# Rough attention scores as pairs of 64-row tiles, and the weighted sums copied out of PSUM by ScalarE

## The chip, the cores and the metric

One core of a Trainium2 chip runs one program. The metric is the device time of one execution in microseconds (us), median of the runs shown.

## The reference, cut to what matters

A 7x7 local-attention convolution is followed by full attention over 3136 tokens of 64 features for each of 4 images, and then by gates and a mixture of experts. The change lies in the attention:

```python
scores = a[:, :, None] + b[:, None, :] + einsum('bif,bjf->bij', x * wc, x)
attn_weight = softmax(scores, axis=2)
attn = einsum('bij,bjf->bif', attn_weight, x)
```

with x the layer-normed tokens (4, 3136, 64). The softmax needs a number near each query's largest score, so that the exponentials stay in range; any such number gives the same quotient.

## The kernel before

`attention` splits the tokens of every image b into 7 chunks of 448 queries (CH) and 25 tiles of 128 keys (NT, the last of 64). Two float16 parts, high and low, stand for a float32 number: `xs` has the high part of the keys in partitions 0 to 63 and the low part in 64 to 127, `vh` and `vl` the projected queries, doubled over both halves of the partitions.

A **step** is one chunk; 28 of them run over 4 images, and one more (`body(B, 0, ...)`) ends the last. Step i does two things at once on TensorE. It makes **rough scores** (L959) of its own queries, whose largest values DVE takes (L1257); they are needed for the next step only. And it **attends** for chunk i-1: exact scores (L970, two matmuls for each key tile), exponential on ScalarE (L1088), weighted sums (L986, float32, two 64-column tiles side by side).

A step has 13 slots of two key tiles (SL). TensorE's order in a slot s: at odd s the sums of two earlier slots, then rough score, two exact matmuls, rough, two exact, and in some slots a third rough score. Steps with 4 query tiles (q = 0, 2, 4, 6 of an image) have 28 rough scores, e = 0 to 27, three to a slot; steps with 3 (q = 1, 3, 5) have 21, two to a slot. They end in slot 9. In slot 10 the maxima are transposed (L1048), in slot 11 the next image's queries are projected (L942; ScalarE L1068 and DVE L1148 copy them out); both use banks of `ps_m`, the 3 banks of the rough scores. Rough score e waits until DVE has reduced e-3; e = 2 waits for L1148 of the step before.

All sums of a chunk gather in one PSUM bank, `ps_a`. The last sums of chunk i-2 are issued in slot 1 of step i. DVE copies the bank out between its reductions (`block_out`, L1239), and the first sums of chunk i-1, in slot 3, wait for that copy:

```python
for back in range(s - LAG - s % 2, s - LAG + 1):
    for a in range(len(tiles(back))):
        sums(m, i - 1, back, a)
...
elif s == 0:
    pe.wait_ge(sums_out, n)
```

SP then gathers the denominators from the copy and moves one half (`denominators`), DVE inverts (`invert`, L1243, L1245), and GpSimd multiplies (`finish`). `steps` runs steps 2 to 5 of an image in a hardware loop.

Of the kernel before, what the change touches and what calls it, by code (L numbers as in the profile page):

```python
# [20 lines left out]
PIX = H * W  # L21
# [623 lines left out]
def attention(nc, tok, tres, xa, xhat, xT, xs, vh, vl, wa, attn, early_added, last_in, t1_dram, in_t, rden_dram):  # L645
# [12 lines left out]
    with ExitStack() as ctx:  # L658
# [10 lines left out]
        MAXIMA = NT * NCH  # L669
        LAST_ROUGH = 9  # L670
        BLOCK_AT, INVERT_AT = 2, 4
# [7 lines left out]
        mpart = sb("at_mpart", [TT, QT, NCH])  # L679
        mtop = sb("at_mtop", [TT, QT])  # L680
        mrow = sb("at_mrow", [QT, TT], F16)
        proj = sb("at_proj", [128, 128])
# [12 lines left out]
        hi = [attn[:, B - PAIRS + t, :].bitcast(F16)[:, 0:PIX] for t in range(PAIRS)]  # L695
        lo = [attn[:, B - PAIRS + t, :].bitcast(F16)[:, PIX:2 * PIX] for t in range(PAIRS)]
        stage = flat[:, 0:2 * CH].rearrange("p (a n) -> p a n", a=2)
        moved_half = flat[:, 2 * CH:4 * CH].rearrange("p (a n) -> p a n", a=2)
# [24 lines left out]
        split = sem("at_split")  # L723
        spread = [sem(f"at_spread{b}") for b in range(B)]
        v_done = sem("at_v_done")
        vh_done = sem("at_vh_done")
# [35 lines left out]
        def steps(eng, body):  # L762
# [13 lines left out]
            body(B, 0, B * NCH, B % 2, None)  # L776

        def query_tiles(b, par):

            return QT if (b + par) % 2 == 0 else QT - 1  # L780
# [4 lines left out]

        def slot_of(e, b, par):

            return min(LAST_ROUGH, e // (query_tiles(b, par) - 1))

# [30 lines left out]
        with nc.Block() as block:  # L820
            @block.sync
            def _(sp):
                for t in range(PAIRS):
                    sp.wait_ge(early_added, t + 1)
                    sp.wait_ge(added, t + 1)
                    sp.dma_start(t1_dram[t], tres[:, t, :]).then_inc(stored[t], 16)
                def stack(t):

                    sp.wait_ge(stored[t], 16)
                    sp.wait_ge(split, NG + t)  # L830
                    for i in range(2):
                        part = slice(64 * i, 64 * i + 64)
                        sp.dma_start(xs[0:64, 2 * t + i, :], hi[t][part, :]).then_inc(spread[2 * t + i], 16)
                        sp.dma_start(xs[64:128, 2 * t + i, :], lo[t][part, :]).then_inc(spread[2 * t + i], 16)

                def maxima(b, q):
                    sp.wait_ge(top_half, q + (b * NCH + 1))
                    at = q * CH + C * (q % 2)
                    whole = QT - 1 if q % 2 or q == NCH - 1 else QT
                    sp.dma_start(vh[127:128, b, at:at + whole * TT].rearrange("p (a t) -> p a t", t=TT),  # L840
                                 mrow[0:whole, :]).then_inc(top_in, 16)
                    if q == NCH - 1:
                        sp.dma_start(vh[127:128, b, PIX - LAST:PIX], mrow[whole:QT, 0:LAST]).then_inc(top_in, 16)

                def denominators(m, k, n):

                    sp.wait_ge(sums_out, n + 1)
                    for a in range(2):
                        sp.dma_start(halves[:, a, :],
                                     stage[64 * a + C - 1:64 * a + C, n % 2, :]  # L850
                                     .rearrange("p (a n) -> p a n", n=DN)).then_inc(gathered, 16)
                    sp.dma_start(moved_half[sum_rows(m), n % 2, :],
                                 stage[sum_rows(m + 1), n % 2, :]).then_inc(half_in, 16)
                    sp.wait_ge(inverted, n + 1)
                    sp.dma_start(rden_dram.rearrange("o (a n) -> (o a) n", n=DN), den[:, :]).then_inc(rden_sent, 16)
                    sp.wait_ge(rden_sent, (n + 1) * 16)
                    if n > 0:
                        sp.wait_ge(divided, n + 2)
                    sp.dma_start(rden[:, :], rden_dram.broadcast_to([128, CH])).then_inc(rden_in, 16)

                stack(0)

                for i in range(B * NCH):
                    if i >= 2:
                        denominators(*divmod(i - 2, NCH), i - 2)
                    maxima(*divmod(i, NCH))
                    if i == 0:
                        stack(1)
                    if i == (B - 1) * NCH:

                        sp.wait_ge(score_done, 2 * NCH * SL)
                        sp.dma_start(tres[:, 0, :], t1_dram[0]).then_inc(in_t[0], 16)
                for i in range(B * NCH - 2, B * NCH):
                    denominators(*divmod(i, NCH), i)
                sp.wait_ge(top_in, 16 * (B * NCH + B))
                sp.wait_ge(rden_in, 16 * B * NCH)

            @block.gpsimd
            def _(pool):
# [22 lines left out]
                pool.memset(mhalf[:, 1:2], -0.5).then_inc(divided, 1)  # L902
                for n in range(B * NCH):
                    finish(*divmod(n, NCH), n, n % 2)

            @block.tensor
            def _(pe):
# [38 lines left out]
                def rough_scores(b, q, i, par, base, e):  # L946
# [7 lines left out]
                    elif e == PROJECT_BANK and not begin and before(b, q, 1)[0] in range(B - 1):  # L954
# [3 lines left out]
                    queries = slice(start, start + w) if isinstance(q, int) else bass.ds(start, w)  # L958
                    pe.matmul(ps_m[0:w, e % RB, 0:CH], vh[:, b, queries], xs[:, b, kb * CH:(kb + 1) * CH],  # L959
                              start=True, stop=True).then_inc(rough_done, 1)  # L960

# [48 lines left out]
                def body(b, q, i, par, base):  # L1010
# [7 lines left out]
                    if b < B and isinstance(q, int) and q == 0:  # L1018
                        pe.wait_ge(spread[b], 32)
                    for s in range(SL):  # L1020
                        rough = [e for e in range(ro) if slot_of(e, b, par) == s]
                        if attend and s >= LAG + 1 and (s % 2 == 1 or s == SL - 1):
# [3 lines left out]
                        elif attend and s == 1 and step != (0, 1):  # L1026
                            for back in range(SL - LAG, SL):
                                for a in range(len(tiles(back))):
                                    sums(late, i - 2, back, a)
                        if rough:  # L1030
                            rough_scores(b, q, i, par, base, rough[0])
                        for a in range(2):
                            if attend and a < len(tiles(s)):
                                if s == 0 and a == 0:
                                    pe.wait_ge(top_in, i * 16 + 16 * b)
                                scores(m, k, i - 1, 1 - par, s, a)
                            if a + 1 < len(rough):
                                rough_scores(b, q, i, par, base, rough[a + 1])
                        if not attend:
# [17 lines left out]

                steps(pe, body)
                for s in range(SL - LAG, SL):
# [4 lines left out]
            def _(act):  # L1064
                def query_half(b, k, u, bank):

                    act.wait_ge(v_done, u + 1)
                    act.activation(vh[:, b, columns_of(k)], bank, ACT.Identity,  # L1068
                                   bias=vbias[:, :]).then_inc(vh_done, 1)

                def body(b, q, i, par, base):
# [3 lines left out]
                    for s in range(SL):  # L1075
# [14 lines left out]
                        else:  # L1090
                            if s < NG:
                                turn_out(1, s)
                            if 0 <= s - BACK_AFTER < NG:
                                turn_back_out(1, s - BACK_AFTER)
                        if s == PROJECT_AT and b < B - 1:
                            query_half(b + 1, q, i + NCH, ps_m[:, PROJECT_BANK, 0:CH])
# [36 lines left out]
                for k in range(NCH):  # L1133
                    query_half(0, k, k, first_bank(k))
                steps(act, body)

            @block.vector
            def _(v):
# [52 lines left out]
                def split_projection():  # L1191
# [3 lines left out]
                    link(v.tensor_copy(proj16[:, 0, :, :], both))  # L1195
                    link(v.tensor_tensor(proj16[:, 1, :, :], both, proj16[:, 0, :, :], ALU.subtract))
                    v.memset(proj16[:, :, 1, C - 1:C], 0.0).then_inc(proj_split, 1)

# [14 lines left out]
                for d in range(2):  # L1213
                    ins = v.tensor_scalar(proj[low, 64 * d:64 * d + 64], mat("drop")[low, 0:64],
                                          vec("wc")[low], None, ALU.mult)
                link(ins)
                v.tensor_copy(proj[low, 63:64], vec("wa")[low]).then_inc(proj_set, 1)
                v.wait_ge(folded, 1)
# [16 lines left out]

                def block_out(n, par):
                    v.wait_ge(sum_done, n * SL + SL)
                    v.wait_ge(divided, n + 1)
                    v.tensor_copy(stage[:, par, :], ps_a[:, 0:CH]).then_inc(sums_out, 1)  # L1239

                def invert(n):
# [5 lines left out]
                def body(b, q, i, par, base):  # L1247
                    step = (b, q) if isinstance(q, int) else None
                    count = query_tiles(b, par) if b < B else 0
                    per = max(1, count - 1)  # L1250
                    block_at, invert_at = per * BLOCK_AT, per * INVERT_AT + 2
                    for e in range(count * NCH if b < B else QT * NCH):
# [6 lines left out]
                        if step == (0, 0) and e % per == per - 1:  # L1259
                            if e // per < NG:  # L1260
                                variance(1, e // per)
                            if 1 <= e // per <= NG:
                                normalize(1, e // per - 1)
                        if e == block_at and step not in ((0, 0), (0, 1)):
                            block_out(i - 2, par)
                        if e == invert_at and step == (0, 1):
# [15 lines left out]
                last = B * NCH - 1  # L1282
                block_out(last, last % 2)
                invert(last)
# [801 lines left out]
```

## Time and profile before

| | us |
|---|---|
| median of 3 runs (lowest, highest) | 2011.94 (2011.4, 2014.27) |
| the profiled execution: time | 2013.85 |
| the profiled execution: span | 2012.1 |
| TensorE busy in the span | 1724.3 |
| VectorE (DVE) busy | 1227.3 |
| ScalarE (ACT) busy | 1165.7 |
| GpSimd (POOL) busy | 660.0 |

A matmul's busy time in the profile includes its way through the array, so that two neighbours overlap; what a matmul costs is read from start to start. The attention lies between 640 and 1450 us of the span.

### The profile page before, as it was taken

How to read it: one execution, taken by the hardware profiler on the slowest of the kernel's cores; microseconds unless marked ns; L12 is line 12 of the kernel's file. 1: busy time of each engine (PE TensorE's matmuls, PEld its weight loads, DVE VectorE, ACT ScalarE, POOL GpSimd, SP SyncE). 2: the span in 40 equal slices, each digit the busy share in tenths (PEclk: the TensorE clock that was granted, in tenths of full speed). 3: DMA queues.
4: the chain of work that ended last, by engine and by line, in shares of the span. 5: the costliest groups of instructions: out<-in, count | busy, mean ns of one | idle time of the engine just before them, and what ended most of it. 6: DMA issues, size and time to landing. Idle time of an engine off the chain costs nothing. (4 is left out here: it accounts for less than half of the span.)

```text
span 2012.1 us, 32023 instructions
## 1 busy us (share of the span) xinstructions
PE 1724.3 (86%) x11589; PEld 609.7 (30%) x11589; DVE 1227.3 (61%) x1736; ACT 1165.7 (58%) x1565; POOL 660.0 (33%) x378
## 2 busy tenths in 40 slices
PE   5468787877765799999999999999885979999998
PEld 1011111111102333333333333333243423333333
DVE  3249999899986766655655566555256444333343
ACT  3799999899723544444444444444354655656664
POOL 0798888888551300000000000000122312222222
PEclk9799999999986899999999999999997989999999
DMA  2220210120132110000000000100011002000000
GB/s 95 84 104 36 81 61 32 71 74 30 61 128 82 33 40 14 14 11 14 14 12 15 15 14 15 45 12 14 19 75 32 1 0 48 8 7 10 7 10 9
DMA packets 25161, 72.89 MB, mean 36 GB/s; under 512 B 5456, under 2 KB 14672, under 8 KB 23632
## 3 DMA queue, kind: packets, MB, share of 16 engines
q1 hardware_dynamic: 24896, 70.28, 10.9%
q8 instruction: 80, 1.31, 0.3%
q10 hardware_dynamic: 144, 0.96, 0.1%
q14 instruction: 41, 0.34, 0.1%
HBM read 47.84 MB, written 13.62 MB: 31 GB/s over the span
## 5 line engine op out<-in xcount | busy, mean ns | idle before, releaser
L1088 ACT ACTIVATE at_prob<-at_ps_s 128x896 f32<-128x896 f32 x336 | 305.9, 917 | 406.7 <-PE at_ps_s L970 406.2
L1257 DVE TENSOR_REDUCE at_mpart<-at_ps_m 128x1 f32<-128x448 f32 (+1 forms) x700 | 399.8, 619 | 194.2 <-PE at_ps_m L959 193.8
L424 DVE TENSOR_TENSOR cm_prod<-cm_ps_ev,win 128x1792 f32<-128x1792 f32 x196 | 388.7, 2018 | 17.5 <-ACT cm_ps_ev L475 9.5
L368 POOL TENSOR_TENSOR cm_diff<-front 128x1792 f32<-128x1792 f32 x98 | 320.7, 3276 | 71.3 <-POOLq L113 38.3
L1710 ACT ACTIVATE ge_hid<-ge_ps,ffn 128x448 f32<-128x448 f32 x448 | 249.6, 634 | 153.7 <-PE ge_ps L1583 153.1
L986 PE MATMUL at_ps_a<-at_prob,win 128*64 128x448 f32 x1344 | 296.4, 554 | 10.1 <-DVE attn L1239 10.1
L581 PE MATMUL cm_ps_acc<-cm_prod,cst 128*32 128x504 f32 x1568 | 221.5, 637 | 76.0 <-DVE cm_prod L424 45.8
L970 PE MATMUL at_ps_s<-vh,front 128*128 (+3 forms) x700 | 248.4, 355 | 1.6 <-DMA vh<-at_mrow 1.6
L970 PE MATMUL at_ps_s<-vl,front 128*128 (+3 forms) x700 | 247.9, 354 | 0.0
L959 PE MATMUL at_ps_m<-front,vh 128*128 128x448 f16 (+1 forms) x700 | 239.8, 357 | 7.7 <-DVE at_mpart L1257 6.9
L895 POOL TENSOR_TENSOR attn<-attn 64x448 f32<-64x448 f32 x28 | 31.6, 1129 | 526.9 <-DMA attn<-attn 526.9
L1561 PE MATMUL ge_ps<-ge_hid,ffn 128*64 128x448 f32 x896 | 198.2, 556 | 0.0
L463 ACT ACTIVATE cm_hid<-cm_ps_hid,cst 128x1792 f32<-128x1792 f32 x98 | 171.0, 1745 | 0.0
L1583 PE MATMUL ge_ps<-attn,w1h 128*128 (+1 forms) x448 | 160.4, 358 | 9.2 <-ACT ge_hid L1710 7.4
L1583 PE MATMUL ge_ps<-attn,w1l 128*128 (+1 forms) x448 | 159.3, 355 | 0.0
L456 ACT ACTIVATE cm_diff<-cm_diff 128x1792 f32<-128x1792 f32 x98 | 147.9, 1509 | 13.7 <-POOL cm_diff L368 13.7
L538 PE MATMUL cm_ps_hid<-cm_diff,cst 32*32 32x448 f32 x2744 | 104.9, 566 | 55.5 <-ACT cm_hid L463 37.8
L1859 DVE COPY ge_wide<-ge_ps 128x448 f32<-128x448 f32 x112 | 69.9, 624 | 124.0 <-PE ge_ps L1570 122.5
L1866 DVE SCALAR_TENSOR_TENSOR ge_part<-ge_ps,ffn,ge_wide 128x448 f32<-128x448 f32 x112 | 76.4, 682 | 106.7 <-PE ge_ps L1561 106.3
L375 POOL TENSOR_TENSOR cm_lg<-cm_lg,cm_topb 128x448 f32<-128x448 f32 x98 | 112.1, 1153 | 47.9 <-DVE cm_topb L409 47.9
L986 PEld LDWEIGHTS at_ps_a<-at_prob,win 128*64 128x64 f32 x1344 | 80.6, 135 | 142.8 <-issue 96.9
L959 PEld LDWEIGHTS at_ps_m<-front,vh 128*128 (+2 forms) x700 | 68.2, 98 | 166.5 <-issue 68.7
(205 smaller groups left out, 1775.4 us busy)
## 6 DMA issues: line engine op xcount, KB each, us to landing
win<-x_dram SPq DMA_DIRECT2D x28, 868.0 KB
at_rden<-rden_dram SPq DMA_DIRECT2D x28, 224.0 KB, 3.3
x_dram<-win SPq DMA_DIRECT2D x4, 962.0 KB
conv_out<-cm_cout SPq DMA_DIRECT2D x28, 112.0 KB, 3.5
win<-x SPq DMA_DIRECT2D x2, 1568.0 KB, 12.5
t_dram<-front SPq DMA_DIRECT2D x2, 1568.0 KB, 6.8
front<-attn SPq DMA_DIRECT2D x8, 392.0 KB, 6.2
attn<-attn SPq DMA_DIRECT2D x28, 112.0 KB, 2.2
```

Source lines behind the costliest of these rows:

```text
L368: pool.tensor_tensor(diff[:, s % ND, 0:n, :].rearrange("p n (r c) -> p n r c", c=W), a.rearrange("p n (r c) -> p n r c", c=W), b, ALU.subt ...
L424: v.tensor_tensor(prod[:, hs, :, 0:CH].rearrange("p s (r c) -> p s r c", c=W), ev.rearrange("p s (r c) -> p s r c", c=W), wv, ALU.mult).th ...
L463: act.activation(hid[0:n, s % 2, :, :], ps_hid[0:n, :, 0:CH], ACT.Relu, bias=vec("t2")[0:n]).then_inc(hrelu_done, 1)
L581: ins = pe.matmul(ps_acc[32 * r:32 * r + 32, hs, 0:CH + EXT], mat("tap_in", 32), prod[:, hs, r, :], start=(k == 0), stop=(k == STEPS - 1), ...
L959: pe.matmul(ps_m[0:w, e % RB, 0:CH], vh[:, b, queries], xs[:, b, kb * CH:(kb + 1) * CH], start=True, stop=True).then_inc(rough_done, 1)
L970: ins = pe.matmul(ps_s[0:w, (s + par) % 2, a, 0:CH], xs[:, m, t * TT:t * TT + w], half[:, m, columns_of(k)], start=(h == 0), stop=(h == 1))
L986: ins = pe.matmul(ps_a[64 * a:64 * a + 64, 0:CH], xT[:, m // 2, t, 64 * i:64 * i + 64], prob_of(s)[:, a, :], start=(t < 2), stop=(t >= NT ...
L1088: act.activation(prob_of(s)[0:w, 0:a, :], ps_s[0:w, (s + 1 - par) % 2, 0:a, 0:CH], ACT.Exp).then_inc(exp_done, 1)
L1257: v.tensor_reduce(mpart[0:w, a, kb:kb + 1], ps_m[0:w, e % RB, 0:CH], AX.X, ALU.max).then_inc(rough_max, 1)
L1561: ins = pe.matmul(ps_o[64 * a:64 * a + 64, ep % 2, 0:CH], mat("w2", n, C), hid[:, j % NHB, :], start=(h == 0), stop=(h == 1), tile_positio ...
L1583: ins = pe.matmul(ps[:, hidden_bank(b, k, j), 0:CH], w[:, n * 128:(n + 1) * 128], own16[b // 2][:, b % 2, columns_of(k)], start=(h == 0), ...
L1710: act.activation(hid[:, j % NHB, :], ps[:, hidden_bank(b, k, j), 0:CH], ACT.Gelu, bias=mat("b1", n, 1)).then_inc(gelu_done, 1)
```

## The change

Rough scores no longer contract over 128 partitions (high and low part of the keys) but over 64, the high part alone, with a `tile_position` of row 0 or row 64. An even e uses partitions 0 to 63, an odd e partitions 64 to 127, and the two stand side by side. The high parts are therefore needed in partitions 64 to 127 too (`xhigh`): three DMAs bring them there (four images, one has them already). The order in a slot is new. The projection keeps its last column in both halves. TensorE's loop is written out. The copy out of `ps_a` moves from DVE to ScalarE, behind the exponential of slot 2 (BLOCK_AT).

```diff
-        LAST_ROUGH = 9
+        again = sb("at_again", [128, PIX], F16)
+        xhigh = [again[64:128, :], hi[0][64:128, :], lo[0][64:128, :], again[64:128, :]]
+        def plain_steps(body):
+            for b in range(B):
+                for q in range(NCH):
+                    body(b, q, ...)
+            body(B, 0, B * NCH, B % 2, None)
+        def rough_pairs(b, par):
+            last = query_tiles(b, par) * NCH if b < B else 0
+            pairs = [range(e, min(last, e + 2)) for e in range(0, last, 2)]
+            extra = [s for s in range(0, SL, 2 if query_tiles(b, par) == QT else SL)]
+            at = sorted([(s, 0) for s in range(SL)] + [(s, 2) for s in extra])
+            return {place: pair for place, pair in zip(at, pairs)}
...
 SP  stack(t), between the high and the low part of i == 0:
+    if t > 0:
+        sp.wait_ge(spread[1], 32)
+    sp.dma_start(xhigh[2 * t], hi[t][part, :]).then_inc(again_in[2 * t], 16)
 SP  loop over steps:
+    if i == NCH:
+        sp.wait_ge(rough_max, MAXIMA)
+        sp.dma_start(xhigh[3], hi[1][64:128, :]).then_inc(again_in[3], 16)
 POOL
+    if n == 2 * NCH:
+        for b in (2, 3):
+            pool.wait_ge(again_in[b], 16)
 PE  rough_scores
-    pe.matmul(ps_m[0:w, e % RB, 0:CH], vh[:, b, queries], xs[:, b, kb * CH:(kb + 1) * CH], ...)
+    half = e % 2
+    rows = slice(64 * half, 64 * half + 64)
+    pe.matmul(ps_m[0:w, e % RB, 0:CH], vh[rows, b, queries], xhigh[b][:, keys] if half else xs[rows, b, keys],
+              start=True, stop=True, tile_position=(64 * half, 0)).then_inc(rough_done, 1)
 PE  body
+    if b != 1:
+        pe.wait_ge(again_in[b], 16)
-    if rough:
-        rough_scores(b, q, i, par, base, rough[0])
+    for e in pairs.get((s, 0), ()):
+        rough_scores(b, q, i, par, base, e)
     for a in range(2):
         ...scores(m, k, i - 1, 1 - par, s, a)
-        if a + 1 < len(rough):
-            rough_scores(b, q, i, par, base, rough[a + 1])
+        for e in pairs.get((s, a + 1), ()):
+            rough_scores(b, q, i, par, base, e)
-    steps(pe, body)
+    plain_steps(body)
 ACT, after the exponential of slot s
+    if s == BLOCK_AT and step not in ((0, 0), (0, 1)):
+        block_out(i - 2, par)
 DVE
-    if e == block_at and step not in ((0, 0), (0, 1)):
-        block_out(i - 2, par)
```

`block_out` itself keeps its two waits and reads `act.copy(stage[:, par, :], ps_a[:, 0:CH]).then_inc(sums_out, 1)`; the one behind the last step moves with it. `split_projection` loses a memset and `proj` gains a one-column copy.

## Rows read from the trace of the kernel before

**Rows 1.** Windows: the attention's steps, busy us (and instructions) of each engine, granted clock.
```profile
698.00:1447.00 749.00, 734.34 (x3539) 280.84 (x3537) 435.40 (x830) 334.83 (x386) 60.98 (x54) 1.00 0.07 18
```
**Rows 2.** Timeline of PE, a four-tile step: slots 2, 3, 5 (start, busy, line).
```profile
1110.02 0.35 PE L970 MATMUL at_ps_s<-vl,front 128*128 x1
1110.21 0.35 PE L959 MATMUL at_ps_m<-front,vh 128*128 128x448 f16 x1
1111.02 1.72 PE L986 MATMUL at_ps_a<-at_prob,win 128*64 128x448 f32 x8 [0.46 <-DVE attn L1239]
1112.67 0.36 PE L959 MATMUL at_ps_m<-front,vh 128*128 128x448 f16 x1
...
1115.42 1.72 PE L986 MATMUL at_ps_a<-at_prob,win 128*64 128x448 f32 x8
```
**Rows 3.** Timeline of PE, a three-tile step: slots 0, 2, 3, 5.
```profile
1131.99 0.36 PE L959 MATMUL at_ps_m<-front,vh 128*128 128x448 f16 x1
...
1136.97 0.35 PE L970 MATMUL at_ps_s<-vl,front 128*128 x1
1137.62 1.72 PE L986 MATMUL at_ps_a<-at_prob,win 128*64 128x448 f32 x8 [0.30 <-DVE attn L1239]
...
1141.65 0.60 PE L986 MATMUL at_ps_a<-at_prob,win 128*64 128x448 f32 x2
```
**Rows 4.** Timeline of PE where rough scores are narrow (64 columns), last chunk of an image.
```profile
851.46 0.35 PE L959 MATMUL at_ps_m<-front,vh 128*64 128x448 f16 x1
851.74 0.36 PE L970 MATMUL at_ps_s<-vh,front 128*128 128x448 f16 x1
851.94 0.35 PE L970 MATMUL at_ps_s<-vl,front 128*128 128x448 f16 x1
852.23 0.38 PE L959 MATMUL at_ps_m<-front,vh 128*64 128x448 f16 x1
```
**Rows 5.** Timeline of PE in the gates: 64-row tiles behind full ones (records of one fp32 pass).
```profile
1482.36 0.61 PE L1489 MATMUL ge_ps<-tok,front 128*128 128x128 f32 x4
1482.89 0.59 PE L1462 MATMUL ge_ps<-win,tok 64*64 64x448 f32 x2
1482.91 0.59 PE L1474 MATMUL ge_ps<-attn,wa 64*64 64x448 f32 x2
```
**Rows 6.** Timeline of DVE and ACT, the same stretch as rows 2, and at the step's end.
```profile
1110.35 0.61 DVE L1239 COPY attn<-at_ps_a 128x448 f32<-128x448 f32 x1
1110.49 0.92 ACT L1088 ACTIVATE at_prob<-at_ps_s 128x896 f32<-128x896 f32 x1 [0.41 <-PE at_ps_s L970]
1113.07 3.35 DVE L1257 TENSOR_REDUCE at_mpart<-at_ps_m 128x1 f32<-128x448 f32 x6 [1.05 <-PE at_ps_m L959]
...
1130.44 0.92 ACT L1088 ACTIVATE at_prob<-at_ps_s 128x896 f32<-128x896 f32 x1 [1.66 <-PE at_ps_s L970]
1131.25 0.63 ACT L1068 ACTIVATE vh<-at_ps_m,at_vbias 128x448 f32 x1
...
1132.06 0.68 DVE L1148 SCALAR_TENSOR_TENSOR vl<-at_ps_m,at_vbias,vh 128x448 f32 x1 [3.74 <-ACT vh L1068]
1132.66 1.15 DVE L1257 TENSOR_REDUCE at_mpart<-at_ps_m 128x1 f32<-128x448 f32 x2
```
**Rows 7.** One tile's instructions: copies out of PSUM on ACT (min/median/max ns).
```profile
L1088 ACT ACTIVATE at_prob_last<-at_ps_s x28: 537/537/537, 727.8 to 1446.6; 64x448 f32<-64x448 f32 x28
L1105 ACT COPY win<-at_ps_s x7: 258/585/586, 674.0 to 690.3; 128x512 f32<-128x512 f32 x6, 64x128 f32<-64x128 f32 x1
```
**Rows 8.** Timeline of PE: the transpose of the maxima in a three-tile step.
```profile
1153.27 0.35 PE L970 MATMUL at_ps_s<-vl,front 128*128 x1
1153.79 0.27 PE L1048 MATMUL at_ps_m<-tok,at_mtop 128*3 128x128 f32 x1 [0.17 <-DVE at_mtop L1274]
```
**Rows 9.** Timeline, the first rough score, and SP's issues ahead of it.
```profile
672.06 0.74 PE L959 MATMUL at_ps_m<-front,vh 128*128 128x448 f16 x3 [0.73 <-ACT vh L1068]
...
664.28 0.59 SPq L833 DMA_DIRECT2D front<-attn  x1
```

More of the change, by code:

```diff
@@ L724, in attention @@
         spread = [sem(f"at_spread{b}") for b in range(B)]
+        again_in = [sem(f"at_again_in{b}") for b in range(B)]
         v_done = sem("at_v_done")
@@ L776, in steps @@
             body(B, 0, B * NCH, B % 2, None)
+        def plain_steps(body):
+            for b in range(B):
+                for q in range(NCH):
+                    body(b, q, b * NCH + q, (b + q) % 2, b * MAXIMA + sum(query_tiles(b, (b + p) % 2) for p in range(q)) * NCH)
+            body(B, 0, B * NCH, B % 2, None)
         def query_tiles(b, par):
@@ L784, in query_rows @@
             return LAST if isinstance(q, int) and q == NCH - 1 and a == QT - 1 else TT
-        def slot_of(e, b, par):
-            return min(LAST_ROUGH, e // (query_tiles(b, par) - 1))
+        def rough_pairs(b, par):
[4 more added lines that the diff above has]
+            return {place: pair for place, pair in zip(at, pairs)}
         def before(b, q, n):
@@ L833, in stack @@
                         sp.dma_start(xs[0:64, 2 * t + i, :], hi[t][part, :]).then_inc(spread[2 * t + i], 16)
+                        if i == 0:
+                            if t > 0:
+                                sp.wait_ge(spread[1], 32)
+                            sp.dma_start(xhigh[2 * t], hi[t][part, :]).then_inc(again_in[2 * t], 16)
                         sp.dma_start(xs[64:128, 2 * t + i, :], lo[t][part, :]).then_inc(spread[2 * t + i], 16)
@@ L958, in rough_scores @@
                     queries = slice(start, start + w) if isinstance(q, int) else bass.ds(start, w)
-                    pe.matmul(ps_m[0:w, e % RB, 0:CH], vh[:, b, queries], xs[:, b, kb * CH:(kb + 1) * CH],
-                              start=True, stop=True).then_inc(rough_done, 1)
+                    half = e % 2
+                    rows = slice(64 * half, 64 * half + 64)
+                    keys = slice(kb * CH, (kb + 1) * CH)
+                    pe.matmul(ps_m[0:w, e % RB, 0:CH], vh[rows, b, queries], xhigh[b][:, keys] if half else xs[rows, b, keys],
+                              start=True, stop=True, tile_position=(64 * half, 0)).then_inc(rough_done, 1)
                 def scores(m, k, n, par, s, a):
@@ L1019, in body @@
                         pe.wait_ge(spread[b], 32)
+                        if b != 1:
+                            pe.wait_ge(again_in[b], 16)
+                    pairs = rough_pairs(b, par)
                     for s in range(SL):
-                        rough = [e for e in range(ro) if slot_of(e, b, par) == s]
                         if attend and s >= LAG + 1 and (s % 2 == 1 or s == SL - 1):
@@ L1069, in query_half, with block_out @@
                                    bias=vbias[:, :]).then_inc(vh_done, 1)
+                def block_out(n, par):
+                    act.wait_ge(sum_done, n * SL + SL)
+                    act.wait_ge(divided, n + 1)
+                    act.copy(stage[:, par, :], ps_a[:, 0:CH]).then_inc(sums_out, 1)
                 def body(b, q, i, par, base):
@@ L1135, in _ @@
                 steps(act, body)
+                last = B * NCH - 1
+                block_out(last, last % 2)
             @block.vector
@@ L1195, in split_projection @@
                     link(v.tensor_copy(proj16[:, 0, :, :], both))
-                    link(v.tensor_tensor(proj16[:, 1, :, :], both, proj16[:, 0, :, :], ALU.subtract))
-                    v.memset(proj16[:, :, 1, C - 1:C], 0.0).then_inc(proj_split, 1)
+                    v.tensor_tensor(proj16[:, 1, :, :], both, proj16[:, 0, :, :], ALU.subtract).then_inc(proj_split, 1)
                 def ones(t):
@@ L1216, in _ @@
                 link(ins)
+                v.tensor_copy(proj[low, 127:128], vec("wa")[low])
                 v.tensor_copy(proj[low, 63:64], vec("wa")[low]).then_inc(proj_set, 1)
@@ L1234, in _ @@
                 ones(0)
[L1236 to L1239, printed above, removed]
                 def invert(n):
@@ L1250, in body @@
                     per = max(1, count - 1)
-                    block_at, invert_at = per * BLOCK_AT, per * INVERT_AT + 2
+                    invert_at = per * INVERT_AT + 2
                     for e in range(count * NCH if b < B else QT * NCH):
@@ L1282, in _ @@
                 last = B * NCH - 1
-                block_out(last, last % 2)
                 invert(last)
```

## The prediction

> **What bounds the kernel now.** I read the windows first, since the change lies in one stage. Over the 749 us in which the attention's steps run, TensorE is busy 734 at the full clock (granted 1.00, which is 2.4 GHz), DVE 435, ScalarE 335, GpSimd 61 [rows 1]. So TensorE sets the end here, and what counts is the time from one matmul's start to the next. That comes from its timeline. A float16 matmul of 448 columns takes 0.19 us (1110.02 to 1110.21), the float32 sums of two slots 1.65 (1111.02 to 1112.67) [rows 2]. The pattern repeats every two slots: 4.40 us in a four-tile step (1111.02 to 1115.42: 1.65, then 14 matmuls and 0.09), and 4.03 in a three-tile step (1137.62 to 1141.65: 12 matmuls) [rows 2, 3]. TensorE has three kinds of hole. It stands at the first sums, waiting for DVE's copy (0.46 us, 0.30 us idle) [rows 2, 3]; a three-tile step waits for the maxima ahead of the transpose, 0.52 instead of 0.19 [rows 8]; and each change of tile shape costs something, which is the number on which this change turns.
>
> **What a change of shape costs.** In an image's last chunk the fourth query tile is 64 columns wide, so its rough scores run in another tile shape than the exact scores around them. Entering that shape takes 0.29 us (851.94 to 852.23) in place of 0.19, leaving it 0.28 (851.46 to 851.74), and the matmul after that comes at 0.20 in place of 0.19 [rows 4]. So 0.10 in and 0.10 to 0.11 out. Is it the same where the rows are cut, not the columns? The nearest rows are in the gates: four records in 0.61 us, the last lasting 0.27 as the transpose's does, are 0.11 apart, so a fifth would start at 1482.80; the 64x64 tiles start at 1482.89, again 0.09 late [rows 5, 8]. They also show the gain: four tiles, two of them in the same columns but other rows, start within 0.02 us of each other and run together [rows 5]. No row has a cut of the rows alone, so the price has two bounds: nothing (if cutting rows needs no stop), and 0.17, what a matmul is still busy after its successor's start (0.35 or 0.36 less 0.19) [rows 2]. I take 0.10, since three measured shapes agree on it. The Trainium skill (TensorEngine Tiling (Array Packing), Key Properties) says that changing the tiling mode drains TensorE, and the trace agrees that each change costs 0.09 to 0.10 us. Its Overview gives up to twice the speed for a contraction of 64; by that alone 344 pairs would save 344 x 0.19 = 65 us, an estimate from that page.
>
> **Pairs instead of singles.** Two rough scores cost 0.38 before. A pair costs 0.19, plus 0.11 to leave, plus 0.10 to enter. So
> - a pair between two exact scores costs 0.40: it loses 0.02;
> - a pair right behind sums (odd s) pays only for leaving: 0.30, gains 0.08;
> - a pair right ahead of sums (place (s, 2) at even s) pays one change that was there anyway: gains 0.09 to 0.10;
> - the single last one of a three-tile step, behind sums, costs 0.30 instead of 0.19.
>
> A four-tile step has 14 pairs and ends in slot 8; a three-tile step has 10 pairs and a single and ends in slot 9.
>
> *Slots 3 to 8.* Four tiles: 1.65 (sums) + 0.30 (pair and leaving) + 0.76 (four exact matmuls) + 0.09 (entering) + 0.30 + 0.76 + 0.09 + 0.19 + 0.09 = 4.23 a period, against 4.40; three periods gain 0.5. Three tiles: 1.65 + 0.30 + 0.76 + 0.09 + 0.30 + 0.76 + 0.09 = 3.95 against 4.03; gain 0.2.
>
> *Slots 9 and 10.* Four tiles: one rough score less, gain 0.2. Three tiles: three singles (0.57) and the transpose's wait (0.33) go, one single at 0.30 comes: gain 0.6. The wait goes because the last reduction begins 0.40 after its matmul (1112.67 to 1113.07) and lasts about 0.6 [rows 2, 6], while 8 exact matmuls (1.5) now follow.
>
> **DVE behind the pairs.** With three banks the second of a pair needs the first of the previous pair reduced: 0.40 + 0.61 + 0.06 (1110.35 + 0.61 to 1111.02) = 1.07 after that pair [rows 2, 6]. The next pair comes 0.30 + 0.57 + 0.28 = 1.15 after it, so there is room, if only 0.08. Six reductions take 3.35 of a period of 4.23 [rows 6], so DVE does not become the bound. One place is too tight: (0, 2). DVE is with L1148 from 1132.06 to 1132.74 and first reduces e = 0 from 1132.66 on [rows 6], done 1133.27; the pair with e = 3 is due 1.15 after slot 0's start at 1131.99 [rows 3], at 1133.14, and must wait to 1133.33. That is 0.2 us in each of steps 1 to 21 (an image still to be projected).
>
> **The copy on ScalarE.** This is where I see the price. ScalarE reaches `block_out` only behind the exponential of slot 2, which needs that slot's last exact score. Call T the start of that matmul. The exponential starts at T + 0.47 (1110.02, 1110.49); what follows it on ScalarE starts 0.81 later (1130.44, 1131.25), though its record lasts 0.92 [rows 2, 6]. No row is a 128x448 copy; a 64-partition 448-column exponential took 0.54, a 512-column copy 0.59 [rows 7]. I take 0.54, and 0.06 back to TensorE as with DVE. The first sums start at T + 0.47 + 0.81 + 0.54 + 0.06 = T + 1.88, whatever else TensorE has by then. Before, they started at T + 1.00 in four-tile steps (1110.02, 1111.02, with a rough score between) and at T + 0.65 in three-tile steps (1136.97, 1137.62) [rows 2, 3]. Behind the waiting sums stand slot 3's pair, its exact scores and so all else; nothing covers it. DVE's freed 0.61 us is worth nothing, since DVE is not the bound.
>
> *Slot 0 to the first sums of slot 3.* Both kinds of step are now alike: (0.30 + 0.76 + 0.09 + 0.19 + 0.09) in slot 0, 1.65 + 0.30 + 0.76 in slot 1, 0.09 + 0.30 + 0.57 to T in slot 2, that is 5.10, and 1.88 behind T: 6.98, or 7.18 with the 0.2 wait on DVE. Before: 5.63 with three tiles (1131.99 to 1137.62) [rows 3]. With four, three more singles (0.57), and from T 0.35 more of which one of those singles is 0.19: 5.63 + 0.57 + 0.16 = 6.36 [rows 2, 3].
>
> **The sum.**
> - Four tiles, with 0.2 wait: 7.18 - 6.36 - 0.5 - 0.2 = +0.1; without (image 3): -0.1. 11 of the one, 4 of the other: +1.
> - Three tiles: 7.18 - 5.63 - 0.2 - 0.6 = +0.7; without the 0.2: +0.5. 8 and 3: +7.4.
> - The closing step without rough scores: its sums started at T + 0.28, now T + 1.88: +1.6. Step 1 has no copy: -0.6.
> - The four last chunks: 7 narrow singles, which change the shape on their own, now stand in pairs that change it anyway: -0.5 each, -2.
> - The start: SP's first DMA is issued at 664.28, the first rough score starts at 672.06, released by ScalarE [rows 9]. One DMA of the same size now stands ahead of the one it needs; it may become the later of the two: +0.5.
> - Nothing: the loop written out (periods are the same in and out of it), GpSimd's waits (its data came steps earlier; 61 us busy [rows 1] cover them), the DMA at step 7 (SP issues it where its wait is met, and next owes a gather with over 1 us of slack), the memset.
>
> Together +8 us. The profiled execution took 2013.85 (span 2012.1, 1.75 around it), so it would be 2022; on the median of 2011.94, 1.9 below it, that is 2020.
>
> **Rivals.**
> - *Cutting the rows needs no stop.* So entering and leaving are free. Counting the changes that the pairs add: 17 in a four-tile step, 15 in a three-tile one, 16 x 17 + 12 x 15 = 452 at 0.10 = 45 us; the 0.2 waits grow by some 4. +8 - 41 = -33, on 2012 that is 1979. It decides where the price falls under 0.07 (12 us by 452): below that the kernel is faster by more than 4 us. For it: no row shows a cut of rows alone. Against: the gates' 0.09. The Trainium skill's sentence on mode switching, above, speaks against it too. Chance 0.12, with a part of it (half price, near 2000) included.
> - *The stop is dearer.* The second tile's weights are loaded one behind the other, or the drain is 0.17: 452 x 0.07 = +32, 2052; for loading, half of that, 2036. Chance 0.15.
> - *The tiles don't overlap* (the change doesn't do what it says): 344 x 0.19 = +65, 2085. The gates speak against it. 0.03.
> - *A quicker copy.* The stall at slot 3 is shorter, because ScalarE's copy is quicker or its start earlier than rows of other shapes say: at 0.3 less in each of 27 steps -8 us: no change, 2012; it decides for "faster" from 0.45 less. Chance 0.2.
> - *My sum*, within some 7 us: 0.5.
>
> **The numbers.** Likeliest 2020, its own range 2014 to 2027. Range 2000 to 2038: it leaves out the free stop below (0.10) and the full drain and no overlap above (0.10). A measurement of this kernel tells 0.2%, 4 us, from no change. Faster (under 2008): the free or half-priced stop 0.12, 0.08 of the quicker copy, 0.03 of my sum. Within: 0.12 of the quicker copy, 0.09 of my sum. Slower (over 2016): 0.38 of my sum, 0.15 and 0.03: 0.56.
>
> **What would show it.** PE's timeline: both of a pair within 0.02 us; 0.28 to 0.30 where a pair is entered and left; the waits list has sums (L986's successor) waiting for ScalarE's copy some 1 us, 27 times, in place of DVE; a rough score in slot 0 waits 0.2 for DVE; the transpose's wait is gone; three- and four-tile steps of nearly one length to slot 3. The forecast is wrong if pairs are entered for less than 0.05, or if the first sums start before T + 1.5.

## The result, and the profile after

The changed kernel takes 2030.41 us (2030.08 to 2031.04), the kernel before 2012.68: a ratio of 1.0088, 95% interval 1.0071 to 1.0106. It is 17.7 us slower; 2020 was forecast, 2014 to 2027 as the likeliest case's own range and 2000 to 2038 as the range. The profiled execution has a span of 2029.2 us, 17.1 more than before.

The timeline shows where it went. First the pairs and the copy, in a three-tile step (the same one as [rows 3], PE, then ACT; start, busy, line):

```profile
1144.12 0.36 PE L990 MATMUL at_ps_m<-front,vh 64*128 64x448 f16 x1
1144.12 0.36 PE L990 MATMUL at_ps_m<-attn,vh 64*128 64x448 f16 x1
1144.41 0.36 PE L1001 MATMUL at_ps_s<-vh,front 128*128 128x448 f16 x1
...
1144.99 0.35 PE L1001 MATMUL at_ps_s<-vl,front 128*128 128x448 f16 x1
1145.27 0.36 PE L990 MATMUL at_ps_m<-front,vh 64*128 64x448 f16 x1
1145.48 0.36 PE L990 MATMUL at_ps_m<-attn,vh 64*128 64x448 f16 x1
1145.77 0.97 PE L1017 MATMUL at_ps_a<-at_prob,win 128*64 128x448 f32 x4
...
1149.45 0.35 PE L1001 MATMUL at_ps_s<-vl,front 128*128 128x448 f16 x1
1151.31 0.60 PE L1017 MATMUL at_ps_a<-at_prob,win 128*64 128x448 f32 x2 [1.51 <-ACT attn L1107]
```
```profile
1149.92 0.92 ACT L1126 ACTIVATE at_prob<-at_ps_s 128x896 f32<-128x896 f32 x1 [0.24 <-PE at_ps_s L1001]
1150.73 0.53 ACT L1107 COPY attn<-at_ps_a 128x448 f32<-128x448 f32 x1
```

The two of a pair start in the same hundredth (1144.12) and the next exact score follows 0.29 later; a pair is entered 0.28 after the last exact score (1144.99, 1145.27). The pair at the end of slot 0 is torn: its second half comes 0.21 late, behind DVE. And the first sums start at T + 1.86 (1149.45, 1151.31), released by ScalarE's copy of 0.53 us behind the exponential. In a four-tile step it is the same 1.86 with the pair in between (sums idle 1.21 before them). Over all steps it is 1.86 in 16, 1.78 in ten and 1.84 in the closing one. The waits list has it 27 times:

```profile
PEld at_ps_m L990 <- DVE at_mpart L1294: 111.0, 235, 1.4
PEld at_ps_a L1017 <- ACT attn L1107: 44.8, 27, 1.9
PE at_ps_a L1017 <- ACT attn L1107: 35.5, 27, 1.5
```

The first of these is idle time of the weight loader alone; TensorE's own idle time for that cause is 1.5 us in the same list. The starts of the 28 transposes measure the steps: the first and the last stand in this view (min/median/max ns, then first and last start), with the last sums below them; first the two rows of the kernel before, then those of the changed one.

```profile
L1048 PE MATMUL at_ps_m<-tok,at_mtop x28: 271/272/273, 697.7 to 1421.4; 128*4 128x128 f32 x16, 128*3 128x128 f32 x12
L986 PE MATMUL at_ps_a<-at_prob_last,win x56: 539/539/590, 730.0 to 1447.6; 128*64 128x448 f32 x56
L1081 PE MATMUL at_ps_m<-tok,at_mtop x28: 271/273/273, 704.1 to 1436.5; 128*4 128x128 f32 x16, 128*3 128x128 f32 x12
L1017 PE MATMUL at_ps_a<-at_prob_last,win x56: 539/539/590, 737.8 to 1464.2; 128*64 128x448 f32 x56
```

So the span's 17.1 us are made of three parts inside the attention, and 0.7 elsewhere:
- the 27 intervals between transposes: 732.4 instead of 723.8, +8.6;
- the closing step, from the last transpose to the last sums: 27.7 instead of 26.2, +1.5;
- **step 0**, from the first rough score (671.4; before 672.06 [rows 9]) to the first transpose: 32.66 instead of 25.62, +7.0, against which the first rough score came 0.7 earlier.

Step 0 was the surprise. It doesn't attend; TensorE instead turns the second pair of images (`turn(1, s)`, one group a slot), ScalarE squares them (L1149) and DVE takes their variance (L1210) after every third reduction. DVE's timeline after:

```profile
678.85 1.68 DVE L1294 TENSOR_REDUCE at_mpart<-at_ps_m 128x1 f32<-128x448 f32 x3
683.24 0.69 DVE L1210 TENSOR_REDUCE at_var<-attn 128x8 f32<-128x512 f32 x1 [2.71 <-ACT attn L1149]
...
687.63 1.68 DVE L1294 TENSOR_REDUCE at_mpart<-at_ps_m 128x1 f32<-128x448 f32 x3
692.01 0.69 DVE L1210 TENSOR_REDUCE at_var<-attn 128x8 f32<-128x512 f32 x1 [2.70 <-ACT attn L1149]
```

Before, DVE ran through the same stretch without a hole:

```profile
678.88 1.68 DVE L1257 TENSOR_REDUCE at_mpart<-at_ps_m 128x1 f32<-128x448 f32 x3
680.48 0.68 DVE L1168 TENSOR_REDUCE at_var<-attn 128x8 f32<-128x512 f32 x1
```

TensorE's timeline after shows what it waited for:

```profile
677.07 0.36 PE L990 MATMUL at_ps_m<-at_again,vh 64*128 64x448 f16 x1 [0.17 <-DVE at_mpart L1294]
677.60 0.55 PE L990 MATMUL at_ps_m<-front,vh 64*128 64x448 f16 x1 [0.17 <-DVE at_mpart L1294]
679.53 0.55 PE L990 MATMUL at_ps_m<-at_again,vh 64*128 64x448 f16 x1 [1.37 <-DVE at_mpart L1294]
680.01 2.07 PE L946 MATMUL at_ps_s<-tok,front 128*128 128x128 f32 x8
```

At 677.60 and 679.53 stand the two of slot 2's second pair, e = 8 and 9. The second needs e = 6 reduced, and in DVE's order e = 6 stands behind a variance. Behind it in TensorE's order stands the turn (680.01) for the next variance, on which DVE then waits 2.7 us. Each waits for the other once every two slots.

### The profile page after: what moved, and what is told of

Read it like the earlier page. It is cut to its first block and busy times, and to the rows that moved or that the text cites. A ratio compares the mean times of both kernels' runs of the same rounds, so it can differ in the third digit from the quotient of the medians.

```text
span 2029.2 us, 31287 instructions
## 1 busy us (share of the span) xinstructions
PE 1714.1 (84%) x11589; PEld 572.6 (28%) x11589; DVE 1225.4 (60%) x1708; ACT 1176.4 (58%) x1593; POOL 659.8 (33%) x378
## 5 line engine op out<-in xcount | busy, mean ns | idle before, releaser
L1001 PE MATMUL at_ps_s<-vh,front 128*128 128x448 f16 (+1 forms) x700 | 251.1, 359 | 1.2 <-DMA vh<-at_mrow 1.2
L1001 PE MATMUL at_ps_s<-vl,front 128*128 128x448 f16 (+1 forms) x700 | 248.1, 354 | 0.0
L990 PE MATMUL at_ps_m<-front,vh 64*128 64x448 f16 (+1 forms) x356 | 129.5, 365 | 4.1 <-DVE at_mpart L1294 3.0
L553 PE MATMUL cm_ps_lg<-cm_hid,cst 128*32 128x448 f32 x784 | 95.1, 555 | 24.1 <-ACT cm_rden L506 8.1
```

The costliest lines, as they stand in the source:

```text
L1001: ins = pe.matmul(ps_s[0:w, (s + par) % 2, a, 0:CH], xs[:, m, t * TT:t * TT + w], half[:, m, columns_of(k)], start=(h == 0), stop=(h == 1))
```

## The experiments

All times are medians; the kernel before took 2012.98 us in the first four runs and 2011.69 in the last four. Intervals are those of the ratio to it; the changed kernel's ratio is to the 2012.68 us of its own comparison. "Steps" is the time from the first to the last transpose in the profiled execution, read as above, which leaves out what varies elsewhere (the part ahead of the first rough score and the part behind the attention each differ by some 3 us between executions of kernels that don't touch them).

| run | us | ratio, 95% interval | steps | first rough score to first transpose |
|---|---|---|---|---|
| before | 2012.98 | | 723.8 | 25.6 |
| changed | 2030.41 | 1.0088 (1.0071 to 1.0106) | 732.4 | 32.7 |
| e1_copy_on_dve | 1993.77 | 0.9908 (0.9892 to 0.9925) | 698.9 | 32.6 |
| e2_copy_alone_on_act | 2036.49 | 1.0119 (1.0102 to 1.0136) | 749.2 | 25.6 |
| e3_turns_first | 2022.94 | 1.0045 (1.0028 to 1.0062) | 731.5 | 26.2 |
| e4_early_copy | 1993.01 | 0.9906 (0.989 to 0.9923) | 696.5 | 33.1 |
| e5_before_early_copy | 1996.32 | 0.9918 (0.9905 to 0.9932) | 711.8 | 25.6 |
| e6_early_copy_turns_first | 1983.78 | 0.9863 (0.9848 to 0.9878) | 695.7 | 26.2 |
| e7_no_pair_at_slot0_end | 1984.23 | 0.9862 (0.9847 to 0.9877) | 694.5 | 25.4 |
| e8_both_on_row_0 | 2043.33 | 1.0157, a single run | 753.0 | 26.0 |

The last column starts late where the turns come first (e3, e6, e7, e8): there the turn of slot 0 stands ahead of the first rough score and is left out. Under e3 step 0 is measured from an earlier point too.

**Copy back on DVE, pairs kept.**
```diff
-                        if s == BLOCK_AT and step not in ((0, 0), (0, 1)):      # ScalarE
-                            block_out(i - 2, par)
+                        if e == block_at and step not in ((0, 0), (0, 1)):      # DVE
+                            block_out(i - 2, par)
```


> The changed kernel with one part undone: the copy out of ps_a is DVE's again, behind the reduction of rough score 6 or 4; the pairs stay. Theory (the copy behind ScalarE's exponential is the loss, 1.86 us from the last exact score of slot 2 to the first sums): three-tile steps start their sums at T + 0.28 (11 x 1.58 = 17 us less), four-tile steps at about T + 0.77 (15 x 1.09 = 16 less), the closing step 1.6 less: about 1995 us. Rival (the pairs with their changes of tile shape are the loss, the copy is innocent): at least 2025 us, and T to the first sums stays what it is in the changed kernel or is made up by waits for DVE. If this is under the kernel before (2012.7), the pairs by themselves gain.

1993.77, as expected. The waits list has 15 waits of four-tile steps left, none over 0.4 us, and none of three-tile steps:
```profile
PEld at_ps_a L1017 <- DVE attn L1272: 5.3, 15, 0.4
```
So the pairs, on their own, make the kernel 19 us faster, though step 0 keeps its 7 us loss; the copy behind the exponential costs 36.6 us of the changed kernel.

**The copy alone on ScalarE.**
```diff
-                        if e == block_at and step not in ((0, 0), (0, 1)):      # DVE
-                            block_out(i - 2, par)
+                        if s == BLOCK_AT and step not in ((0, 0), (0, 1)):      # ScalarE
+                            block_out(i - 2, par)
```


> The kernel before with the copy alone moved to ScalarE, behind the exponential of slot 2; no pairs. Theory: the first sums start at T + 1.86 instead of T + 1.00 (15 four-tile steps) and T + 0.65 (11 three-tile steps), and T + 0.28 in the closing step: 12.9 + 13.3 + 1.6 = 28 us more, about 2040. Rival (copy innocent): 2013, as before.

2036.49, 23.5 over before. The steps grew by 25.4 (26.2 expected without the closing step) and the closing step by 1.5; that the whole grew by 3.4 less lies in the parts ahead of the attention and behind it, and is within their spread. The move alone is worse than the whole change.
```profile
PE at_ps_a L986 <- ACT attn L1074: 35.6, 26, 1.5
L1048 PE MATMUL at_ps_m<-tok,at_mtop x28: 271/272/273, 696.8 to 1446.0; 128*4 128x128 f32 x16, 128*3 128x128 f32 x12
```
In the steps the two parts alone give -24.9 and +25.4, which would add up to +0.5; together they gave +8.6. The missing 8.1 us are those that the pairs gain at the first sums when the copy isn't there: on DVE, T to the sums falls from 0.65 to 0.28 in 11 three-tile steps and from 1.00 to 0.73 in 15 four-tile steps, 4.1 + 4.0 = 8.1. Behind the exponential it is 1.78 to 1.86 with the pairs and without them.

**The turns of step 0 ahead of its rough scores.**
```diff
+                        if not attend:                 # TensorE's order in a slot
+                            if s == 0:
+                                pe.wait_ge(vl_done, NCH)
+                            if s < NG:
+                                turn(1, s)
                         for e in pairs.get((s, 0), ()):
                             rough_scores(b, q, i, par, base, e)
...
-                            if s == 0:
-                                pe.wait_ge(vl_done, NCH)
-                            if s < NG:
-                                turn(1, s)
```


> The changed kernel with one edit in step 0 alone: each slot's turn of the second pair of images is issued ahead of the slot's rough scores, not behind them. Theory (step 0 grew from 25.6 to 32.7 us because the second pair of rough scores in even slots waits for a reduction that stands behind DVE's variance, and the next turn, which the next variance needs, stands behind that pair): step 0 back to about 26 us, DVE's waits for ScalarE's squares (7.6 us) gone, and with TensorE less idle the half clock at its end shorter: 7 to 9 us less, about 2022. Rival (the added DMAs or the half clock itself lengthen the stage): step 0 stays over 31 us and the time at 2030.

2022.94, 7.5 less than the changed kernel. DVE's holes of 2.7 us are gone (one of 0.75 is left), and step 0 takes 26.2 us from its first rough score:
```profile
683.12 1.91 DVE L1295 TENSOR_REDUCE at_mpart<-at_ps_m 128x1 f32<-128x448 f32 x3
684.96 0.68 DVE L1211 TENSOR_REDUCE at_var<-attn 128x8 f32<-128x512 f32 x1
685.67 0.17 DVE L1212 TENSOR_SCALAR at_var<-at_var 128x8 f32<-128x8 f32 x1
```
But that interval flatters the edit, since the first rough score now stands behind a turn and starts at 673.5, not 671.4. From the start of ScalarE's last copy of a projection (L1102 at 670.8; 670.3 in the changed kernel, 671.4 before) to the first transpose it is 28.8 us, against 33.7 in the changed kernel and 26.3 before. So 4.9 of 7.4 us came back in step 0, and 0.9 more in step 1; the rest of the 7.5 lies behind the attention, within its spread. The order of the turns was the larger part of the cause, with the added DMAs still there; the 2.5 us that are left have no single cause shown. Part of the expectation failed: TensorE still ran partly at the half clock there (mean granted clock 0.70 over 671 to 705, in the changed kernel 0.74).

**The copy ahead of the exponential of slot 1.**
```diff
                             n = i - 1
+                            if s == 1 and step != (0, 1):
+                                block_out(i - 2, par)
                             act.wait_ge(score_done, n * SL + s + 1)
...
-                        if s == BLOCK_AT and step not in ((0, 0), (0, 1)):
-                            block_out(i - 2, par)
```


> The changed kernel with the copy on ScalarE, but ahead of the exponential of slot 1, not behind that of slot 2. ScalarE idles there, and the last sums of the chunk before are done. Theory (the place in ScalarE's order is the loss, not the engine): no wait at the first sums, T + 0.28 in three-tile and T + 0.57 in four-tile steps (a pair stands between): 11 x 1.58 + 15 x 1.29 + 1.6 = 38 us less, about 1992. Rival (ScalarE is too slow a place for the copy anywhere): exponentials are pushed back, the exact scores wait for them, and no more than half of it comes back, over 2010.

1993.01, 37.4 less than the changed kernel (38 expected). ScalarE waits for the late sums and copies at once; at the first sums nothing is left (1023.95 to 1024.53 is the pair alone):
```profile
1022.02 0.53 ACT L1107 COPY attn<-at_ps_a 128x448 f32<-128x448 f32 x1 [1.21 <-PE at_ps_a L1017]
1023.18 0.92 ACT L1128 ACTIVATE at_prob<-at_ps_s 128x896 f32<-128x896 f32 x1 [0.63 <-PE at_ps_s L1001]
```
```profile
1023.95 0.35 PE L1001 MATMUL at_ps_s<-vl,front 128*128 128x448 f16 x1
1024.23 0.36 PE L990 MATMUL at_ps_m<-front,vh 64*128 64x448 f16 x1
1024.24 0.36 PE L990 MATMUL at_ps_m<-attn,vh 64*128 64x448 f16 x1
1024.53 0.97 PE L1017 MATMUL at_ps_a<-at_prob,win 128*64 128x448 f32 x4
```
It is the place in ScalarE's order that costs, not the engine.

**The kernel before with the early copy**, the same edit without pairs.

> The kernel before, no pairs, with the copy on ScalarE ahead of the exponential of slot 1. Theory (the copy's place counts, and the kernel before already loses to DVE's copy): the first sums no longer wait: 15 x 0.52 + 11 x 0.37 = 12 us less than before, about 2001. Rival (DVE's copy was harmless, the gain of the early copy came with the pairs): 2012.

1996.32, 15.4 less than before, 12.0 of it in the steps (711.8 against 723.8), which is the expected number; no sums wait for a copy. In the profiled execution another 3 us lie ahead of the first rough score (669.1, before 672.06) and are taken as spread.

**Both mends together.**

> The changed kernel with both mends: the copy ahead of the exponential of slot 1, and in step 0 the turns ahead of the rough scores. Theory (the two losses are independent): 1993.0 less the 7.5 that the turns gave = 1985.5. Against the kernel before with the early copy (about 2001) this gives what the pairs themselves are worth with nothing waiting for the copy: by my terms 15 us, most of it from slots 3 to 10, the transpose's wait and the narrow tiles. Rival (changes of tile shape eat the pairs' gain): within 4 us of that kernel.

1983.78. It is 28 us (1.4%) faster than the kernel before and 12.5 faster than that with the early copy alone, so the rival falls. In the steps the pairs are worth 711.8 - 695.7 = 16.1 us, where my terms gave 15.

**No pair at the end of slot 0**, on top of both mends.
```diff
-            extra = [s for s in range(0, SL, 2 if query_tiles(b, par) == QT else SL)]
+            extra = [s for s in range(2, SL, 2 if query_tiles(b, par) == QT else SL)]
```


> As the one with both mends, and the pair at the end of slot 0 moved to the end of slot 2 (three tiles) or the list shifted by one place (four tiles). Theory (that pair waits 0.2 us for DVE, which comes from the projection's low part, in steps 1 to 21): 21 x 0.2 = 4 us less than the one with both mends, about 1981.5, and the waits list has no rough score waiting for DVE there. Rival (DVE is late by the same amount at the next pair): no difference.

1984.23: no difference. The wait in slot 0 did go, but in four-tile steps, where the last pair is now in slot 9, the transpose waits in its place:
```profile
PEld at_ps_m L1082 <- DVE at_mtop L1310: 4.2, 15, 0.3
```
Where no projection stands ahead (the last image) the steps of four tiles even grew, from 25.7 to 25.9 us. The other four-tile steps grew by up to 0.16. Three-tile steps fell from 25.37 to 25.17 us, the expected 0.2, in six cases, by 0.04 in two and not at all in the last image. So the 0.2 us wait is real, and my expectation overlooked that 14 pairs without slot 0's end reach into slot 9. The steps as a whole fell by 1.2 us, but 1.6 of that is step 1 alone (24.6 instead of 26.2), where the granted clock was higher; more on it below. The other 26 intervals grew by 0.4.

**Both halves on row 0**, so that no two can overlap.
```diff
-                    half = e % 2
+                    half = 0
```


> As the one with both mends, but odd rough scores too use partitions 0 to 63 and tile row 0: the same number of matmuls of the same shape in the same order, but no two can stand side by side. Theory (overlap is real and worth one matmul's 0.19 us for each of 344 pairs): 65 us less those pairs that stand under a wait: 55 to 65 us over the one with both mends, 2041 to 2050, starts of a pair 0.19 apart. Rival (the order alone makes the gain, overlap adds little): under 2000.

2043.33, 59.5 over the kernel with both mends; the steps took 57.2 more. Overlap is real and worth about 0.17 us a pair (57.2 over the 330 pairs of these steps; some stand under DVE's wait). Without it, 64-row tiles lose 41 us in the steps against the plain rough scores of e5 (753.0 against 711.8).
```profile
1000.50 0.35 PE L1001 MATMUL at_ps_s<-vl,front 128*128 128x448 f16 x1
1000.78 0.55 PE L990 MATMUL at_ps_m<-front,vh 64*128 64x448 f16 x2
1001.26 0.36 PE L1001 MATMUL at_ps_s<-vh,front 128*128 128x448 f16 x1
```

## Why the prediction was right, and where not

**The direction and the main mechanism held.** Shown by e1, e2 and e4: the copy behind slot 2's exponential holds the first sums to T + 1.86, in ten steps T + 1.78 (forecast T + 1.88), and costs 37 us.

**The price of a change of shape** was forecast from narrow columns and 64x64 tiles [rows 4, 5] at 0.10 in and 0.10 to 0.11 out. With only the rows cut it is 0.28 in place of 0.19 to enter and 0.29 to the next exact score. The rival of a free stop is refuted, and so is the dearer one. The Trainium skill (TensorEngine Tiling (Array Packing), Key Properties) says that changing the tiling mode drains TensorE. The rows agree as far as each change cost about 0.1 us. By the speedup of up to 2 that the Trainium skill gives for a dimension of at most 64 (same page, Overview), the 344 pairs would save 65 us, an estimate. The measured worth of the pairs in the steps is 16.1 (e6 against e5): the overlap gives 57.2 (e8 against e6), and the same order of 64-row tiles without overlap costs 41.2 (e8 against e5), near the 45 us counted for 452 changes at 0.10.

**The steps.** For steps 2 to 27 the terms gave +1 + 7.4 - 2 = +6.4. (The 7.4 was added up wrongly: 8 x 0.7 + 3 x 0.5 is 7.1. And of the 15 four-tile steps 12 wait on DVE, not 11.) Measured, the 26 intervals behind the first grew by 8.6 - 1.4 = 7.2. Three-tile steps grew by 0.5 to 0.8 (forecast 0.5 and 0.7), four-tile steps by 0 to 0.2 (-0.1 and 0.1), the last chunks shrank by 0.2 to 0.35 (forecast 0.4 to 0.6). The closing step: +1.6 forecast, +1.5 measured. The 0.2 us behind DVE at (0, 2) and the end of the transpose's wait are there as forecast; the copy took 0.53 against 0.54.

**What failed is the term "The start", +0.5.** It priced a DMA, which cost nothing to be seen: the first rough score was released by ScalarE as before. But step 0 itself was given no term, and it grew by 7.0 us. I had costed the new order of pairs only for steps that attend; in step 0 the turns stand behind the pairs, and e3 shows that this makes the larger part of the loss: 4.9 of the 7.4 us that step 0 grew from ScalarE's last copy of a projection. I had looked for who is queued behind a waiting rough score in the typical step, and not in the one that runs other work.

**Step 1** was forecast at -0.6 and measured at +1.4 (27.1 instead of 25.7 from transpose to transpose). In it the granted clock is 0.81 on average, before 0.87, in the windows of the two intervals:
```profile
704.00:731.00 27.00, 24.24 (x100) 7.46 (x101) 16.35 (x26) 12.14 (x12) 0.00 (x0) 0.81 0.31 66
```
Set beside the runs with the turns first, the interval goes with the clock: 27.1 us at 0.81, 26.2 at 0.83 (e3, e6), 24.6 at 0.87 (e7):
```profile
696.60:721.23 24.63, 22.58 (x100) 7.24 (x101) 16.43 (x25) 12.22 (x12) 0.00 (x0) 0.87 0.35 74
```
At the clock that the kernel before had there (0.87, 25.7 us), step 1 with pairs is thus 1.0 us shorter, near the forecast 0.6. So the 2 us are most likely those of the lower clock, which the prediction had no term for. No run changed the clock alone, and e7 also moves a pair.

**The sum.** +8 forecast, +17.7 measured, +17.1 in the profiled executions. Of the 9.1 us between 8 and 17.1, step 0 has 7.0, step 1 has 2.0 and steps 2 to 27 have 0.8; the first rough score, 0.7 earlier instead of 0.5 later, takes back 1.2, and the rest is under 1. The likeliest case's own range (to 2027) missed the time by 3 us. That the time lies in the wide range owes nothing to foresight of step 0: the upper part of the range was drawn for dearer changes of shape (2036 in the milder case), which did not come. Here the range was lucky.

## What to carry to other kernels

Ask of a copy that frees a PSUM bank what stands ahead of it in its engine's order: the same 0.53 us cost 37 us behind one exponential and nothing ahead of the one before. Small tiles side by side paid here only where a change of shape was due anyway, next to another tiled group: a pair between two full matmuls took 0.58 us from the start of the one before to the start of the one behind, two full rough scores 0.57. And when an order is rewritten, walk through the first step by itself: it runs other work in the same slots, and its slack is another.

## What the runs showed of the hardware

- Two 64-row tiles on different rows mostly started 0.003 to 0.004 us apart, and a pair then cost one matmul's 0.19 us plus its changes of shape, also when the two read different tiles of SBUF. Both on the same row (e8) started 0.20 apart.
- Any change among 128x128, 128x64, 64x128 and 64x64 cost 0.09 to 0.12 us of start-to-start time (0.28 to 0.31 between starts in place of 0.19), whichever dimension was cut. The transposes, 3 or 4 columns wide, cost nothing to enter: they started 0.19 behind an exact score where nothing else held them.
- TensorE's granted clock fell to its half level, 1.2 GHz, for part of step 0 in the kernels with pairs: the mean was 0.74 over 671.4 to 704.0 where the same work before kept 1.00. Its waits alone don't explain that: of idle times over 0.6 us in this stretch there were five (the longest 1.92), but the kernel before had five too (the longest 1.24), and with the turns first (e3) there were two (the longest 1.57) and the mean was 0.71 (673.5 to 699.7). What in the new order lowers it, and what that costs in step 0, was not measured. The window of the changed kernel:
```profile
671.40:704.00 32.60, 23.84 (x103) 15.09 (x103) 24.72 (x59) 10.25 (x21) 12.82 (x9) 0.74 0.08 17
```
